# A mixture-of-experts and attention layer on one core: the setup of the weights laid out in another order

## The chip, the cores and the metric

One core of one Trainium2 chip. The metric is the device time of one execution in microseconds (us); smaller is better.

## The reference, cut to what matters

The input is 4 x 1024 tokens of 256 numbers in float32. Three residual steps follow each other: a mixture-of-experts layer of 32 experts (8 chosen for each token, further cut by a threshold), attention (16 heads of 16, 4 key/value heads, rotary tables), and the same mixture-of-experts layer again.

```
x = L0_attn_x
x = x + 0.5 * ffn(layernorm(x), gate_weight, gate_up_proj, down_proj)
x = x + attn(layernorm(x), Wq, Wk, Wv, Wo)
x = x + 0.5 * ffn(layernorm(x), gate_weight, gate_up_proj, down_proj)

logits = x @ gate_weight.T; probs = softmax(logits); top 8; keep until cumulated share 0.8; renormalise
for each expert: gu = x @ w_gu.T; g, u = split(gu); h = silu(g) * u; acc += h @ w_d.T * ce[:, None]
```

## The kernel before, in words

The 4096 tokens are 32 tiles of 128, held in `X` in SBUF (SBUF is the on-chip memory of 128 partitions) for the whole run. Four tiles make a group of 512 tokens, so there are 8 groups, and each is taken twice (two mixture layers), with attention between and beside them. A group is worked in two halves of 256 tokens, and a half in 12 slots. A slot `d` computes gate and up of two chunks of 128 hidden units (`gate_or_up`, 24 matmuls, L1015), then `down` of slot `d - 2` (12 matmuls, L1031). Between them ACT takes the tanh of the gate (`gate`, L578), DVE makes `gated` (L831) and `product` (L839), POOL multiplies by the tokens' combine weights (`weigh`, L508), ACT rounds to a high half (`high`, L585) and POOL subtracts for a low half (`low`, L513). Every product of matrices is made of float16 halves: high times high, high times low and low times high (`PASSES`). There are 384 slots. In the loop `for d in range(-1, SLOTS + 2)` each engine has its own list, written out by hand: slots, attention visits (from slot 64 on) and events. Semaphores alone tie the engines together.

Ahead of the loop stands the setup. The weights come as float32 and have to be scaled by a power of two and split into a float16 high half and a low half. In the order of the code:

- SP loads `st_gu` (gate and up weights, 12288 numbers on each partition) in two transfers, then all of `X` (L343, L344). ACT's queue loads the five small weights `st_g`, `st_q`, `st_k`, `st_v`, `st_o` and then the identity matrix (L553, L554). The down weights `st_d` (6144 numbers) have their place in the arena, a stretch of SBUF shared by staging and by the work buffers of the loop, and SP loads them (L348) only when gate/up and the small weights are split.
- DVE waits for the identity, takes the largest absolute value of each small weight (L679) and of the gate/up weights (L681). POOL reduces these over the partitions (L478, `partition_all_reduce`). DVE makes powers of two from them (`power_of_two`, L686 to L690) and factors for later (L700 to L704).
- `split_weights` (L693, L694) makes both halves on DVE: a `tensor_scalar` for the high one, a `scalar_tensor_tensor` for the low one. It runs for the small weights and then for all gate/up weights in one piece.
- The down weights follow: load, maximum (L714), reduction (L480), scale, both halves.
- Then come the memsets of `vb`, the norm of group 0 in four pieces (L738 to L750 and L734), with a power by POOL between them (`inverse_roots`, L485), the rounding of its rows (ACT L561, POOL L490), their transposition on PE (L966) and its copies on ACT (L566), the router's logits (L975), and routing in seven pieces on DVE (`route`, L763 to L799). SP writes the combine weights out and spreads them over the partitions (`write_combine`, L357, and `spread`, L368).
- PE waits for all splits before its first instruction (L1158 to L1161).

## Time and profile before

| | |
|---|---|
| median of 3 runs | 2420.05 us (2419.04 to 2420.05) |
| the profiled execution's own time | 2418.05 us |
| its span in the profile | 2416.3 us |
| PE busy (matmuls) | 2280.5 us, 94% |
| DVE busy | 1577.1 us, 65% |
| ACT busy | 1215.7 us, 50% |
| POOL busy | 1044.5 us, 43% |
| HBM traffic | 64.25 MB read, 12.85 MB written |

PE is TensorE, DVE is VectorE, ACT is ScalarE, POOL is GpSimd; SP only issues transfers. PEld is the loading of weights into PE, beside its matmuls. A line such as L1015 is the line of the kernel that issued the instruction. The span is the profiler's time from the first instruction to the last, and the execution's own time includes a little around it. Busy shares are averages over the whole span. Times in the timeline and in the chain count from the span's start.

### The profile page before, as it was taken

How to read it: one execution, taken by the hardware profiler on the slowest of the kernel's cores; microseconds unless marked ns; L12 is line 12 of the kernel's file. 1: busy time of each engine (PE TensorE's matmuls, PEld its weight loads, DVE VectorE, ACT ScalarE, POOL GpSimd, SP SyncE). 2: the span in 40 equal slices, each digit the busy share in tenths (PEclk: the TensorE clock that was granted, in tenths of full speed). 3: DMA queues.
4: the chain of work that ended last, by engine and by line, in shares of the span. 5: the costliest groups of instructions: out<-in, count | busy, mean ns of one | idle time of the engine just before them, and what ended most of it. 6: DMA issues, size and time to landing. Idle time of an engine off the chain costs nothing.

```text
span 2416.3 us, 48432 instructions
## 1 busy us (share of the span) xinstructions
PE 2280.5 (94%) x19616; PEld 1517.7 (63%) x19616; DVE 1577.1 (65%) x3099; ACT 1215.7 (50%) x1953; POOL 1044.5 (43%) x863
## 2 busy tenths in 40 slices
PE   0199999999999999999999999999999999999999
PEld 0188886555556556655555655555555655588887
DVE  6545556977777777777777777676776773345443
ACT  0123332156655656656666656666666665633332
POOL 0066664344343444344343433433433433366665
PEclk9999999999999999999999999999999999999999
DMA  5111112101110101111011011101101010011010
GB/s 191 54 36 29 34 37 58 29 14 31 31 30 19 48 21 37 31 25 41 11 37 37 18 33 28 32 3 39 31 21 30 13 29 19 11 37 28 19 37 19
DMA packets 96327, 80.24 MB, mean 33 GB/s; under 512 B 40292, under 2 KB 88676, under 8 KB 95720
## 3 DMA queue, kind: packets, MB, share of 16 engines
q1 hardware_dynamic: 95240, 76.09, 11.2%
q8 instruction: 155, 2.54, 0.4%
q10 hardware_dynamic: 864, 1.05, 0.1%
q14 instruction: 68, 0.56, 0.1%
HBM read 64.25 MB, written 12.85 MB: 32 GB/s over the span
## 4 chain that ended last, share of the span: by engine, by line
PE 90%; DVE 6%; DMA 2%; issue 1%; SPq 0%; POOL 0%; ACT 0%; ACTq 0%; POOLq 0%; DVEq 0%
PE PS L1015 41%; PE PS L1031 21%; PE PS L1043 11%; PE PS L1074 11%; PE PS L989 2%; DVE arena L854 1%; PE PS L1055 1%; PE PS L966 1%; PE PS L992 1%; PE PS L1113 1%; DMA ident<-ident_c 1%; PE PS L1099 1%; DVE WGU L694 1%; DVE amax L681 1%; PE PS L975 0%
## 5 line engine op out<-in xcount | busy, mean ns | idle before, releaser
L1015 PE MATMUL PS<-XT,WGU 128*128 128x256 f16 x9216 | 1117.6, 274 | 11.3 <-DVE arena L831 3.7
L1015 PEld LDWEIGHTS PS<-XT,WGU 128*128 128x128 f16 x9216 | 875.0, 98 | 242.7 <-issue 132.2
L513 POOL TENSOR_TENSOR arena<-arena 128x512 f16<-128x512 f32 x384 | 444.6, 1158 | 1199.8 <-ACT arena L585 1199.8
L854 DVE TENSOR_REDUCE arena<-PS 128x1 f32<-128x512 f32 x1024 | 658.2, 685 | 370.0 <-PE PS L1043 368.0
L608 ACT ACTIVATE arena<-PS,fac 128x512 f32<-128x512 f32 x1024 | 646.3, 684 | 235.8 <-PE PS L1055 234.5
L578 ACT ACTIVATE arena<-PS,fac 128x512 f32<-128x512 f32 x384 | 263.9, 687 | 763.0 <-PE PS L1015 763.0
L1031 PE MATMUL PS<-WD,arena 128*128 128x256 f16 x4608 | 569.4, 274 | 6.5 <-POOL arena L513 6.3
L1031 PEld LDWEIGHTS PS<-WD,arena 128*128 128x128 f16 x4608 | 432.4, 98 | 146.8 <-issue 89.5
L508 POOL TENSOR_TENSOR arena<-arena 128x512 f32<-128x512 f32 x384 | 487.3, 1269 | 49.3 <-DVE arena L839 27.7
L831 DVE SCALAR_TENSOR_TENSOR arena<-arena,PS 128x512 f32<-128x512 f32 x384 | 261.4, 681 | 295.9 <-ACT arena L578 295.4
L1043 PE MATMUL PS<-arena 48*128 48x512 f16 x1024 | 312.2, 382 | 7.2 <-DMA arena<-k_scratch 4.5
L1055 PE MATMUL PS<-arena 50*128 50x512 f16 x1024 | 308.9, 382 | 0.0
L839 DVE SCALAR_TENSOR_TENSOR arena<-arena,PS 128x512 f32<-128x512 f32 x384 | 263.8, 687 | 34.7 <-PE PS L1015 19.1
L1074 PE MATMUL PS<-arena 128*32 128x512 f32 x2048 | 272.9, 605 | 0.0
L585 ACT ACTIVATE arena<-arena 128x512 f16<-128x512 f32 x384 | 241.3, 628 | 12.2 <-POOL arena L508 12.2
L1043 PEld LDWEIGHTS PS<-arena 48*128 48x128 f16 x1024 | 58.3, 94 | 268.8 <-issue 205.6
L966 PE MATMUL PS<-ident,XS 128*128 128x128 f16 x384 | 30.2, 223 | 104.5 <-ACT XS L561 103.2
L966 PEld LDWEIGHTS PS<-ident,XS 128*128 128x128 f16 x384 | 25.1, 99 | 109.3 <-issue 106.4
L566 ACT ACTIVATE XT<-PS 128x1024 f16<-128x1024 f16 x48 | 49.1, 1023 | 54.1 <-PE PS L966 54.1
L1074 PEld LDWEIGHTS PS<-arena 128*32 128x32 f32 x2048 | 40.3, 108 | 54.0 <-issue 28.9
L1055 PEld LDWEIGHTS PS<-arena 50*128 50x128 f16 x1024 | 57.0, 94 | 21.0 <-issue 18.7
L490 POOL TENSOR_TENSOR XS<-XN,XS 128x1024 f16<-128x1024 f32 x24 | 51.1, 2129 | 4.7 <-ACT XS L561 4.7
(111 smaller groups left out, 842.6 us busy)
## 6 DMA issues: line engine op xcount, KB each, us to landing
arena<-ce_scratch SPq DMA_DIRECT2D x256, 128.0 KB, 3.2
arena<-wgu SPq DMA_DIRECT2D x2, 3072.0 KB, 14.9
arena<-q_scratch SPq DMA_DIRECT2D x96, 64.0 KB, 2.2
X<-x SPq DMA_DIRECT2D x1, 4096.0 KB, 31.2
arena<-ktab_c SPq DMA_DIRECT2D x16, 256.0 KB, 4.2
q_scratch<-arena SPq DMA_DIRECT2D x32, 128.0 KB, 1.7
out<-X SPq DMA_DIRECT2D x8, 512.0 KB, 3.0
arena<-wd SPq DMA_DIRECT2D x1, 3072.0 KB, 10.0
```

Of the source, the lines that this page charges most:

```text
L508: pool.tensor_tensor(t, t, c, ALU.mult).then_inc(w_done, 1)
L513: pool.tensor_tensor(hs[1][:, d % HS, :], tw[d % 2], hs[0][:, d % HS, :], ALU.subtract).then_inc(lo_done, 1)
L578: act.activation(z_f, PS[:, B_G, :], ACT.Tanh, scale=F_TANH).then_inc(z_done, 1)
L608: act.activation(pex[:, v % RING * 2 + half, :], PS[:, B_EXP + half, :], ACT.Exp, scale=F_EXP).then_inc(exp_done, 1)
L831: dve.scalar_tensor_tensor(z_f, z_f, 1.0, PS[:, B_G, :], ALU.add, ALU.mult).then_inc(v_done, 1)
L839: dve.scalar_tensor_tensor(tw[d % 2], z_f, G_U_UP, PS[:, B_U, :], ALU.mult, ALU.mult).then_inc(t_done, 1)
L854: dve.tensor_reduce(mx[:, half * REP * QT + c:half * REP * QT + c + 1], PS[:, B_MAX + half, :], AX_X, ALU.max).then_inc(max_taken, 1)
L1015: ins = pe.matmul(PS[:, b, j * HALF_G:(j + 1) * HALF_G], WGU[w][:, kt, part * CHUNKS + c + j, :], XT[r][:, k % 2, kt, half * HALF_G:(half ...
L1031: ins = pe.matmul(PS[:, B_Y, i * HID:(i + 1) * HID], hs[r][:, d % HS, at:at + P], WD[w][:, d % PER_HALF * 2 + j, :], start=(first and j == ...
L1043: pe.matmul(PS[:, B_MAX + half, :], qst[64 * par:64 * par + 48, slot, i, t * P:(t + 1) * P], kst[64 * par:64 * par + 48, slot, half * 512: ...
L1055: pe.matmul(PS[:, B_EXP + n % 2, :], kst[64 * par:64 * par + 50, slot, k * P:(k + 1) * P], qst[64 * par:64 * par + 50, slot, head // 2, ha ...
L1074: ins = pe.matmul(PS[32 * head:32 * head + 32, B_O, :], vst[:, u % 2, k, :], pex[:, (2 * q + r // 2) % RING * 2 + r % 2, :], start=(k == 0 ...
```

## The change

The setup and its waits are written anew; the loop over the slots keeps its instructions.

- SP loads the rows of groups 0 and 1 first (1 MB), then gate/up in two transfers with a semaphore each, then the down weights at once, into the part of `X` whose rows come last. The remaining rows (3 MB) are loaded when the down weights are split. The identity is now first on ACT's queue.
- The arena is carved in another order: the work buffers of the slots (`CB`, `z_f`, `tw`, `hs`) stand at its end, behind the staging of the gate/up weights.
- Maxima, reductions and scales are made in three rounds: small weights, gate/up, down.
- The norm of group 0 and the first piece of its routing stand ahead of the gate/up maximum; the other pieces are between the maxima.
- High halves, but for the router's, are made on ACT (`activation` with Identity and a scale); low halves stay on DVE.
- The gate/up weights are split in four pieces of three slots each, an instruction for each of the two row blocks. ACT makes piece 0, the down weights, and pieces 1 to 3. DVE makes piece 0 and the down weights ahead of the loop, and pieces 1 to 3 behind the products of slots 0 to 2.
- PE waits for each piece where it needs it. The `vb` memsets and the transfers of `kneg` move into the loop, to slot 4.

```diff
-        (cb_f, z_f, t_all, hi_f, lo_f, kcos, ksin, rb, qo_hi, qo_lo, vb_f,
-         qst_f, kst_f, vst_f, pe_f, oT, otok_f, osp_hi, osp_lo, mx, rd_f, ml, mlT) = carve(
-            [(2 * 4 * HALF_G, F32), (GROUP, F32), (2 * GROUP, F32), (HS * GROUP, F16), (HS * GROUP, F16)]
-            + [(GROUP, F32)] * 3 + [(2 * GROUP, F16)] * 2 + [(GT * KV * 32, F32)]
+        assert n_d == (TILES - 2 * GT) * HID
+        st_d = X[:, 2 * GT:, :].rearrange("p t h -> p (t h)")
+        in_pieces = st_gu.rearrange("p (k t q n) -> p q k t n", k=KT, t=2, q=PIECES)
+        hi_pieces, lo_pieces = (w.rearrange("p k (t q c) m -> p q k t (c m)", t=2, q=PIECES) for w in WGU)
+
+        (kcos, ksin, rb, qo_hi, qo_lo, vb_f, qst_f, kst_f, vst_f, pe_f, oT, otok_f, osp_hi, osp_lo, mx, rd_f, ml, mlT,
+         cb_f, z_f, t_all, hi_f, lo_f) = carve(
+            [(GROUP, F32)] * 3 + [(2 * GROUP, F16)] * 2 + [(GT * KV * 32, F32)]
             + [(QKV * 2 * SEQ, F16), (QKV * SEQ, F16), (2 * QT * 32, F32), (RING * 2 * 512, F32), (512, F32),
                (QT * P, F32), (QT * P, F16), (QT * P, F16), (2 * REP * QT, F32), (QT * REP, F32),
...
@@ -338,17 +345,12 @@
         @block.sync
         def _(sp):
+            x_rows = x.rearrange("(i p) h -> p i h", p=P)
+            sp.dma_start(X[:, 0:2 * GT, :], x_rows[:, 0:2 * GT, :]).then_inc(x_in, 16)
             for k in range(KT):
                 n = n_gu // KT
-                sp.dma_start(st_gu[:, k * n:(k + 1) * n], wgu[:, k * n:(k + 1) * n]).then_inc(gu_in, 16)
-            sp.dma_start(X[:, :, :], x.rearrange("(i p) h -> p i h", p=P)).then_inc(x_in, 16)
-
-            sp.wait_ge(gu_split, 1)
-            sp.wait_ge(small_split, 1)
+                sp.dma_start(st_gu[:, k * n:(k + 1) * n], wgu[:, k * n:(k + 1) * n]).then_inc(gu_in[k], 16)
             sp.dma_start(st_d, wd).then_inc(d_in, 16)
-            sp.wait_ge(d_split, 1)
-            for par in range(2):
-                sp.dma_start(kst[64 * par + 48:64 * par + 50, :, :], kneg_c).then_inc(const_rows, 16)
             def write_combine(k):
...
+                if d == PIECES:
+                    sp.wait_ge(gu_split, PIECES)
+                    for par in range(2):
+                        sp.dma_start(kst[64 * par + 48:64 * par + 50, :, :], kneg_c).then_inc(const_rows, 16)
                 if d % 6 == 2 and (d + 4) % PER_GROUP and d + 4 < SLOTS:
                     spread((d + 4) // 6)
...
             pool.wait_ge(consts_set, 1)
-            pool.wait_ge(amax_all, 1)
-            pool.partition_all_reduce(wmax[:, :], amax[:, :], P, ABSMAX).then_inc(wmax_all, 1)
-            pool.wait_ge(amax_d, 1)
-            pool.partition_all_reduce(wmax[:, S_D:S_D + 1], amax[:, S_D:S_D + 1], P, ABSMAX).then_inc(wmax_d, 1)
+            pool.wait_ge(amax_small, 1)
+            pool.partition_all_reduce(wmax[:, S_G:N_SCALES], amax[:, S_G:N_SCALES], P, ABSMAX).then_inc(wmax_small, 1)
...
+            pool.wait_ge(amax_gu, 1)
+            pool.partition_all_reduce(wmax[:, S_GU:S_GU + 1], amax[:, S_GU:S_GU + 1], P, ABSMAX).then_inc(wmax_gu, 1)
+            pool.wait_ge(amax_d, 1)
+            pool.partition_all_reduce(wmax[:, S_D:S_D + 1], amax[:, S_D:S_D + 1], P, ABSMAX).then_inc(wmax_d, 1)
             for d in range(-1, SLOTS + 2):
...
         def _(act):
+            act.dma_start(ident[:, :], ident_c).then_inc(const_in, 16)
             for v, src in ((st_g, wg), (st_q, wq), (st_k, wk), (st_v, wv), (st_o, wo)):
                 act.dma_start(v, src).then_inc(small_in, 16)
-            act.dma_start(ident[:, :], ident_c).then_inc(const_in, 16)
             def rows_high(i):
...
                     take_tokens(n, j, bank)
-            act.wait_ge(scales_set, 1)
             rows_high(0)
+            act.wait_ge(scales_small, 1)
+            for i, v, w in ((S_Q, st_q, WQ), (S_K, st_k, WK), (S_V, st_v, WV)):
+                act.activation(flat(w[0]), v, ACT.Identity, scale=up[:, i:i + 1])
+            act.activation(flat(WO[0]), st_o, ACT.Identity, scale=up[:, S_O:S_O + 1]).then_inc(small_hi, 1)
             take_rows(0, 0, 0, B_O)
             take_rows(0, 0, 1, B_O)
             exponentials(0)
+            act.wait_ge(scales_gu, 1)
+            for q in range(PIECES):
+                for k in range(KT):
+                    ins = act.activation(hi_pieces[:, q, k], in_pieces[:, q, k], ACT.Identity, scale=up[:, S_GU:S_GU + 1])
+                ins.then_inc(gu_hi, 1)
+                if q == 0:
+                    act.wait_ge(scales_d, 1)
+                    act.activation(flat(WD[0]), st_d, ACT.Identity, scale=up[:, S_D:S_D + 1]).then_inc(d_hi, 1)
             for d in range(-1, SLOTS + 2):
                 k, s = divmod(d, PER_GROUP)
                 if d + 1 < SLOTS:
...
-            dve.wait_ge(small_in, 16 * len(small))
-            for s, v in small:
-                link(dve.tensor_reduce(amax[:, s:s + 1], v, AX_X, ALU.max, apply_absolute_value=True))
-            dve.wait_ge(gu_in, 32)
-            dve.tensor_reduce(amax[:, S_GU:S_GU + 1], st_gu, AX_X, ALU.max, apply_absolute_value=True)\
-               .then_inc(amax_all, 1)
+            def amax_of(i, v):
...
+
             mul = ALU.mult
-            link(dve.tensor_scalar(F_TANH, wmax[:, S_GU:S_GU + 1], 0.5 / XW, None, mul))
-            link(dve.tensor_scalar(F_LOGIT, wmax[:, S_G:S_G + 1], 1 / XW, None, mul))
-            link(dve.scalar_tensor_tensor(F_EXP, wmax[:, S_Q:S_Q + 1], HD ** -0.5 / 64, wmax[:, S_K:S_K + 1],
-                                          mul, mul))
-            link(dve.scalar_tensor_tensor(F_O, wmax[:, S_V:S_V + 1], 2.0 ** -18, wmax[:, S_O:S_O + 1], mul, mul))
-            link(split_weights(S_G, st_g, flat(WG[0]), flat(WG[1])))
...
-
-            link(dve.scalar_tensor_tensor(F_T, wmax[:, S_GU:S_GU + 1], 2.0 ** -10, wmax[:, S_GU:S_GU + 1], mul, mul))
-            dve.tensor_scalar(F_Y, F_T, wmax[:, S_D:S_D + 1], None, mul).then_inc(scales_set, 1)
-            split_weights(S_D, st_d, flat(WD[0]), flat(WD[1])).then_inc(d_split, 1)
-            dve.wait_ge(scales_set, 1)
-            dve.wait_ge(d_split, 1)
+            def split_small():
+
+                dve.wait_ge(small_hi, 1)
+                link(low_weights(S_Q, st_q, flat(WQ[0]), flat(WQ[1])))
+                link(low_weights(S_K, st_k, flat(WK[0]), flat(WK[1])))
+                link(low_weights(S_V, st_v, flat(WV[0]), flat(WV[1])))
+                low_weights(S_O, st_o, flat(WO[0]), flat(WO[1])).then_inc(small_split, 1)
+
+            def split_piece(q):
+
+                dve.wait_ge(gu_hi, q + 1)
+                for k in range(KT):
+                    ins = low_weights(S_GU, in_pieces[:, q, k], hi_pieces[:, q, k], lo_pieces[:, q, k])
+                ins.then_inc(gu_split, 1)
...
-            dve.memset(vb[:, :, :, HD:HD + 1], 1.0).then_inc(vb_set, 1)
-            dve.wait_ge(vb_set, 2)
+            dve.wait_ge(small_in, 16 * len(small))
+            for i, v in small[:-1]:
+                link(amax_of(i, v))
+            amax_of(*small[-1]).then_inc(amax_small, 1)
             dve.wait_ge(x_in, 16)
-            for piece in range(4):
-                norm(0, 0, piece)
-            for piece in range(7):
-                route(0, piece, B_O)
+            norm(0, 0, 0)
+            norm(0, 0, 1)
+            dve.wait_ge(wmax_small, 1)
+            link(power_of_two(S_G, N_SCALES))
+            dve.tensor_scalar(flat(WG[0]), st_g, up[:, S_G:S_G + 1], None, mul).then_inc(scales_small, 1)
+            dve.wait_ge(scales_small, 1)
+            low_weights(S_G, st_g, flat(WG[0]), flat(WG[1])).then_inc(g_split, 1)
+            link(dve.tensor_scalar(F_LOGIT, wmax[:, S_G:S_G + 1], 1 / XW, None, mul))
+            norm(0, 0, 2)
+            norm(0, 0, 3)
+            link(dve.scalar_tensor_tensor(F_EXP, wmax[:, S_Q:S_Q + 1], HD ** -0.5 / 64, wmax[:, S_K:S_K + 1],
+                                          mul, mul))
+            link(dve.scalar_tensor_tensor(F_O, wmax[:, S_V:S_V + 1], 2.0 ** -18, wmax[:, S_O:S_O + 1], mul, mul))
+            split_small()
+            route(0, 0, B_O)
+            dve.wait_ge(gu_in[0], 16)
+            link(dve.tensor_reduce(amax[:, S_GU:S_GU + 1], st_gu[:, 0:n_gu // KT], AX_X, ALU.max,
+                                   apply_absolute_value=True))
+            dve.wait_ge(gu_in[1], 16)
+            link(dve.tensor_reduce(pad[:, :], st_gu[:, n_gu // KT:], AX_X, ALU.max, apply_absolute_value=True))
+            dve.tensor_tensor(amax[:, S_GU:S_GU + 1], amax[:, S_GU:S_GU + 1], pad[:, :], ALU.max).then_inc(amax_gu, 1)
+            for piece in range(1, 4):
+                route(0, piece)
+            dve.wait_ge(wmax_gu, 1)
+            link(power_of_two(S_GU, S_GU + 1))
+            link(dve.tensor_scalar(F_TANH, wmax[:, S_GU:S_GU + 1], 0.5 / XW, None, mul))
+            dve.scalar_tensor_tensor(F_T, wmax[:, S_GU:S_GU + 1], 2.0 ** -10, wmax[:, S_GU:S_GU + 1], mul, mul)\
+               .then_inc(scales_gu, 1)
+            dve.wait_ge(d_in, 16)
+            amax_of(S_D, st_d).then_inc(amax_d, 1)
+            for piece in range(4, 7):
+                route(0, piece)
+            dve.wait_ge(wmax_d, 1)
+            link(power_of_two(S_D, S_D + 1))
+            dve.wait_ge(scales_gu, 1)
+            dve.tensor_scalar(F_Y, F_T, wmax[:, S_D:S_D + 1], None, mul).then_inc(scales_d, 1)
+            split_piece(0)
+            dve.wait_ge(scales_d, 1)
+            dve.wait_ge(d_hi, 1)
+            low_weights(S_D, st_d, flat(WD[0]), flat(WD[1])).then_inc(d_split, 1)
             for d in range(-1, SLOTS + 2):
                 k, s = divmod(d, PER_GROUP)
                 if d % PER_HALF == 1 and d > 1:
@@ -930,6 +973,13 @@
                 if d + 1 < SLOTS:
                     gated(d + 1)
                     product(d + 1)
+                if d + 2 < PIECES:
+                    split_piece(d + 2)
+                if d == PIECES:
+                    dve.memset(vb_f, 0.0).then_inc(vb_set, 1)
+                    dve.wait_ge(vb_set, 1)
+                    dve.memset(vb[:, :, :, HD:HD + 1], 1.0).then_inc(vb_set, 1)
+                    dve.wait_ge(vb_set, 2)
                 if (d, 1) in VISIT:
                     visit(VISIT[d, 1])
                 if len(EVENTS[d]) > 1:
...
                 b, done = ((B_G, g_done), (B_U, u_done))[part]
                 if d:
                     pe.wait_ge((v_done, t_done)[part], d)
...
                 first, last = d % PER_HALF == 0, d % PER_HALF == PER_HALF - 1
...
-            pe.wait_ge(const_rows, 32)
             transpose_rows(0, 0, B_O)
             pe.wait_ge(xt_hi, 1)
             transpose_rows(0, 1, B_O)
             pe.wait_ge(xt_lo, 1)
+            pe.wait_ge(g_split, 1)
             logits(0, B_O)
```

**ACT, from its first arithmetic to slot 1.** A row is the line, the operation, the tiles written and read, and their size. Before (L561 is the rounding of group 0's rows, L566 the transposed copies, L571 the router's exponential, L578 tanh, L585 a slot's high half):

```order
L561 ACT_TABLE_LOAD
L561 ACTIVATE XS<-XN 128x1024
L566 ACTIVATE XT<-PS 128x1024 x2
L571 ACTIVATE pr<-ld,fac 128x4x32
L578 ACTIVATE arena<-PS,fac 128x512 x2
L585 ACTIVATE arena<-arena 128x512
```

Now (L572, L577, L582, L589 and L596 are those five):

```order
L572 ACT_TABLE_LOAD
L572 ACTIVATE XS<-XN 128x1024
L641 ACTIVATE WQ<-arena,up 128x1024
L641 ACTIVATE WK<-arena,up 128x256
L641 ACTIVATE WV<-arena,up 128x128
L642 ACTIVATE WO<-arena,up 128x512
L577 ACTIVATE XT<-PS 128x1024 x2
L582 ACTIVATE pr<-ld,fac 128x4x32
L649 ACTIVATE WGU<-arena,up 128x2x768 x2
L653 ACTIVATE WD<-X,up 128x6144
L649 ACTIVATE WGU<-arena,up 128x2x768 x6
L589 ACTIVATE arena<-PS,fac 128x512 x2
```

Four small high halves now stand between the rows' rounding and their transposed copies, and nine large ones between the router's exponential and the first tanh.

**DVE, from the last factor to slot 3** (L836 is `gated`, L844 `product`). Now:

```order
L962 TENSOR_SCALAR fac<-fac,wmax 128x1
L711 SCALAR_TENSOR_TENSOR WGU<-arena,up,WGU 128x2x768 x2
L711 SCALAR_TENSOR_TENSOR WD<-X,up,WD 128x6144
L836 SCALAR_TENSOR_TENSOR arena<-arena,PS 128x512
L844 SCALAR_TENSOR_TENSOR arena<-arena,PS 128x512
L711 SCALAR_TENSOR_TENSOR WGU<-arena,up,WGU 128x2x768 x2
L836 SCALAR_TENSOR_TENSOR arena<-arena,PS 128x512
L844 SCALAR_TENSOR_TENSOR arena<-arena,PS 128x512
```

Two more pieces follow in the same way, behind slots 1 and 2. Before, all splitting (L693, L694) stood ahead of the norm and routing, and slots followed each other with nothing between.

**POOL, from its start to slot 0.** An `ISA` row without tiles is an instruction that changes the loaded library; one with tiles is the reduction over the partitions. In brackets is what an instruction waits for. Before (L508 is `weigh`):

```order
L478 ISA
L478 ISA wmax<-amax 128x8 [waits amax_all,consts_set]
L480 ISA wmax<-amax 128x1 [waits amax_d]
L485 ISA
L485 TENSOR_TENSOR rs<-var,mhalf 128x4 [waits var_ready]
L490 TENSOR_TENSOR XS<-XN,XS 128x1024 [waits xs_hi]
L508 TENSOR_TENSOR arena<-arena 128x512 [waits cb_in0,t_done]
```

Now (L515 is `weigh`):

```order
L487 ISA
L487 ISA wmax<-amax 128x6 [waits amax_small,consts_set]
L492 ISA
L492 TENSOR_TENSOR rs<-var,mhalf 128x4 [waits var_ready]
L497 TENSOR_TENSOR XS<-XN,XS 128x1024 [waits xs_hi]
L534 ISA
L534 ISA wmax<-amax 128x1 [waits amax_gu]
L536 ISA wmax<-amax 128x1 [waits amax_d]
L515 ISA
L515 TENSOR_TENSOR arena<-arena 128x512 [waits cb_in0,t_done]
```

The power (L485, now L492) stood behind both reductions and now stands between the first and the second, and the changes of library are four where they were two.

## Rows read from the trace of the kernel before

**Rows 1.** The page: shares of the engines, and the chain by engine.

```profile
PE 2280.5 (94%) x19616; PEld 1517.7 (63%) x19616; DVE 1577.1 (65%) x3099; ACT 1215.7 (50%) x1953; POOL 1044.5 (43%) x863
...
PE 90%; DVE 6%; DMA 2%; issue 1%; SPq 0%; POOL 0%; ACT 0%; ACTq 0%; POOLq 0%; DVEq 0%
```

**Rows 2.** Two stretches: us, busy us (instructions) by engine, clock, DMA share, GB/s.

```profile
0.00:131.59 131.59, 17.67 (x125) 13.11 (x126) 74.32 (x102) 8.00 (x10) 8.73 (x13) 0.96 0.34 120
131.59:2416.30 2284.71, 2262.79 (x19492) 1504.64 (x19490) 1502.80 (x2997) 1207.68 (x1943) 1035.80 (x851) 1.00 0.11 28
```

**Rows 3.** The chain in order of time (start us, us, what).

```profile
3.65 18.63 DMA ident<-ident_c
...
25.57 12.96 DVE amax L681
...
52.97 13.03 DVE WGU L694
...
76.10 6.56 DVE amax L714
...
135.67 2.62 PE PS L1015 x24
```

**Rows 4.** DMA queues (q1 SP, q10 ACT), 6 to 14 us: packets, MB, share.

```profile
q1 hardware_dynamic: 130, 2.80, 81.5%
q10 hardware_dynamic: 130, 0.47, 14.3%
```

**Rows 5.** Stretches as in rows 2; the last two figures: DMA share, GB/s.

```profile
1.00:2.00 1.00, 0.00 (x0) 0.00 (x0) 0.07 (x2) 0.00 (x0) 0.00 (x0) 1.00 0.85 197
...
14.00:16.00 2.00, 0.00 (x0) 0.00 (x0) 0.00 (x0) 0.00 (x0) 0.00 (x0) 1.00 1.02 436
...
28.00:30.00 2.00, 0.00 (x0) 0.00 (x0) 2.00 (x1) 0.00 (x0) 0.00 (x0) 1.00 1.10 348
```

**Rows 6.** Timeline, DVE's setup: start us, us, engine line op out<-in [idle <-releaser].

```profile
22.57 2.97 DVE L679 TENSOR_REDUCE amax<-arena 128x1 f32<-128x64 f32 x5
...
39.18 0.17 DVE L686 TENSOR_SCALAR wmax<-wmax 128x8 f32<-128x8 f32 x1 [0.66 <-POOL wmax L478]
```

**Rows 7.** Timeline, norm of group 0 and its high rows.

```profile
95.23 1.41 DVE L738 BATCH_NORM_STATS2 stats<-X 128x6 f32<-128x256 f32 x4
...
98.45 0.16 DVE L747 TENSOR_TENSOR nw<-rs 128x4 f32<-128x4 f32 x1 [1.19 <-POOL rs L485]
...
99.25 1.38 DVE L734 TENSOR_SCALAR XN<-X,mv,rstd 128x256 f32<-128x256 f32 x4
100.71 1.28 ACT L561 ACT_TABLE_LOAD   x1 [100.71 <-DVE XN L734]
102.00 1.06 ACT L561 ACTIVATE XS<-XN 128x1024 f16<-128x1024 f32 x1
```

**Rows 8.** Timeline, ACT's high half of slot 0.

```profile
126.93 0.63 ACT L585 ACTIVATE arena<-arena 128x512 f16<-128x512 f32 x1 [7.30 <-POOL arena L508]
```

**Rows 9.** Timeline, transposed copy and routing of group 0.

```profile
104.25 1.02 ACT L566 ACTIVATE XT<-PS 128x1024 f16<-128x1024 f16 x1 [1.19 <-PE PS L966]
...
110.08 0.29 DVE L770 TENSOR_TENSOR pr<-pr,r 128x128 f32<-128x128 f32 x1
...
115.22 0.31 DVE L799 STREAM_TRANSPOSE combT<-comb 128x128 f32<-128x128 f32 x1
```

**Rows 10.** Timeline, the same multiplication in the loop.

```profile
2297.49 1.24 DVE L770 TENSOR_TENSOR pr<-pr,r 128x128 f32<-128x128 f32 x1
```

**Rows 11.** Timeline of POOL, second reduction and power.

```profile
82.75 0.38 POOL L480 PARTITION_ALL_REDUCE wmax<-amax  x1 [43.60 <-DVE amax L714]
97.35 1.06 POOL L485 TENSOR_TENSOR rs<-var,mhalf 128x4 f32<-128x4 f32 x1 [14.22 <-DVE var L744]
```

**Rows 12.** Stretches as in rows 2 (third figure from the end: clock).

```profile
118.00:120.00 2.00, 2.00 (x12) 1.39 (x10) 0.34 (x1) 0.69 (x1) 0.00 (x0) 0.50 0.15 25
```

**Rows 13.** Timeline, PE's first `down`.

```profile
128.84 2.74 PE L1031 MATMUL PS<-WD,arena 128*128 128x256 f16 x12 [4.66 <-POOL arena L513]
```

56 lines of the change are left out of this document (27 added, 29 removed).

## The prediction

> **What bounds the kernel now.** First read the engines' shares and the chain that ended last. TensorE (PE) is busy 94% of the span and carries 90% of the chain [rows 1]. The two stretches then say where the other tenth lies: up to 131.59 us PE has worked 17.67 us of 131.59, behind it 2262.79 of 2284.71 [rows 2]. So the time is a setup of some 131 us, in which PE waits, and a stream of matmuls that is full. The change touches only the setup, and the stream issues the same matmuls after it, so I ask one thing: how much earlier does the stream begin? The chain in order of time shows the setup as one file of steps: the constant's landing at 22.28, the maximum of the gate/up weights, their two halves, the wait for the down weights, their maximum, their halves, and only then the first group's rows [rows 3]. Its last row is my mark: gate and up of slot 4 start at 135.67. They sit on a chain of matmuls from the first `down` on; in the changed kernel I look for the same slot.
>
> **When the small weights are in (call it S).** Before, `ident` is issued at 3.65 and lands 18.63 us later [rows 3]. The two queues share engines: from 6 to 14 us each served 130 packets, but 2.80 MB went to SP's queue and 0.47 to ACT's [rows 4]. One small packet goes per large one of the 3 MB loads. Now SP's first load is 1 MB of rows, in packets of 1 KB like the later part of the 4 MB load, which runs at 348 GB/s [rows 5]. ACT's five weights and `ident` are another 1.05 MB. Together 2.1 MB at 348 GB/s are 6.0 us; data flow from within the second us on [rows 5], say 1.6, so the lower end is S = 7.6. ACT's last issue comes at about 3.7 and some of its packets may still meet the large ones. A packet of those is a 24 KB row of one partition, 0.9 us at a sixteenth of 436 GB/s [rows 5]. If all of `wo`'s share (128 rows, 8 for each of 16 engines) waits for one each, that is 7.2 us more, an upper end of about 15; the old 22.5 is the rival's. I take S = 9, near the lower end, since the byte count of the rows is nearly that of the small weights and they end together.
> The skill's rule speaks against this. The Trainium skill (DMA: Bandwidth & Descriptors, Queues, rings and completion order) says an engine changes between queues only after a packet of some 9 to 17 descriptors. By that the large loads could hold the small queue for a whole turn, and S would stay near the old one. The trace counts one for one [rows 4] and decides for me; the rule is rival A.
>
> **The chain from S on, step by step** (where I can, durations are distances between rows, so that gaps are in them).
> DVE: five small maxima, 22.57 to 25.57, 3.0 [rows 3, 6]; norm pieces 0 and 1, from 95.23 to 97.26 (98.45 less the idle 1.19), 2.0 [rows 7]; four scale steps of 0.17 and some 0.04 between them, 0.85 [rows 6], and three more small ones for `WG` and a factor, about 0.25 each: S+6.7. Norm pieces 2 and 3, 98.45 to 100.63, 2.2 [rows 7]: S+8.9. ACT: table load and high rows, 2.35 and a start of 0.1 [rows 7]: S+11.3. Then the four small high halves. ACT's price per column comes from two rows, 1024 columns in 1.06 and 512 in 0.63 [rows 7, 8]: 0.84 ns per column on 0.2 us. So 1024, 256, 128 and 512 columns cost about 2.6: S+13.9. From the first transposed copy, 104.25, to the multiplication of routing piece 1, 110.08, are 5.8 [rows 9]; the exponential and two small steps, 1.0, belong behind piece 0, so its end is 4.8 after the copy's start: S+18.7. DVE's four low halves (1920 columns at 13.03/12288, 1.06 ns [rows 3], and four starts, 3.0) lie beside it, and so are free.
> The gate/up maximum is 12.95 in one piece [rows 3]; in two, with one more joining step, 13.3: S+32.0. Its bytes are in by 7.6 plus 6.3 MB at the 409 GB/s of [rows 4], 23 us, and it starts its second half at S+25, so the load is hidden; the down weights follow by 31 and are wanted at S+36. Routing pieces 1 to 6 took from 109.5 to 115.53, 6.0 [rows 9], about half of it ahead of the gate/up scales and half behind the down maximum; scales and two factors 1.3; down maximum 6.6 [rows 3]; scales and `F_Y` 1.0: S+46.9.
> Now ACT is what is late. It holds, in its order, `WD` high (6144 columns, 5.4) and six half pieces of `WGU` (1536 columns, 1.5 each, 9.0) ahead of the first tanh: S+61.4. DVE's first piece (a quarter of 13.03, 3.3) and `WD` low (6.6) end at S+59 and are hidden by it. The combine weights' way out and back ends by S+56: before, from 115.53 to slot 0's high half at 126.93 are 11.4, with 1.27 of `weigh` among them [rows 8, 9]. Tanh, gated and product are 0.69 each, like all of their kind: S+63.6.
> Then DVE alternates: piece 1, slot 1, piece 2, slot 2, piece 3, slot 3. A piece is 3.3 and a slot's two products 1.45. And here is a cost that the setup's rows don't show, since POOL stood idle then. The same multiplication takes 0.29 alone and 1.24 beside POOL's work [rows 9, 10]: two SBUF inputs on DVE wait while POOL has the port. Each piece is two such instructions and meets POOL's `weigh` and `low`. Ends: none, or two holds of 1.25 for each piece; I take one, since `weigh` is asked for as a piece's first half starts and so comes between the halves. 3 x (3.3+1.25) + 2 x 1.45 = 16.6: S+80.2, and slot 3's gated product ends at S+80.9. Slot 4 starts at S+81.0, against 135.67. Without anything more that is 54.7 - S, 45.7 us earlier.
>
> **POOL's reload** is what the change adds. Its order now goes reduction, power, subtraction, reduction, reduction, weighing, with a library instruction at each change: three behind the first, where there was one. Only the first of them is exposed: the first reduction ends at S+3.7 (0.66 passes for DVE between a maximum and the scale step [rows 6]), the power is wanted by S+5.1 and its result by DVE at S+6.7. The trace of before has this change of code inside a gap: from 83.13 to 97.35 POOL shows nothing, and then the power waits only for DVE's `var` [rows 11]. So its length is between nothing and 14.2. In between I have no nearer row and take the middle, 7: power ready at S+3.7+7+1.1, 5.1 us later than DVE wants it. Ends: 0 and 12.3. The other two lie in DVE's 13 us maximum and in ACT's 14 us of high halves; if they took over 14 us they would show too.
> The Trainium skill (GPSIMD Engine Reference, Instruction dispatch) gives about 6 us for the first call of freshly loaded code; an estimate from that page is 4.1 us lost instead of 5.1, and the forecast would be 1 us lower.
>
> **Clock.** Before, at 116 to 120 us PE's granted clock was 0.50 (1.2 GHz) and the first `down`, 12 matmuls, took 2.74 behind an idle time of 4.66, where 24 matmuls take 2.62 at 135.67 [rows 3, 12, 13]. In the changed kernel PE works in pieces between DVE's long instructions up to slot 4, so it may begin at 1.2 GHz: 0 to 2.8 lost, I take 1.5.
> **Costless.** The 3 MB of remaining rows are issued at S+59, about 9 us, while group 2's norm comes at slot 33, over 100 us later. SP's next transfer, the second spread, queues behind them but is wanted only by slot 6, some 20 us on. The two memsets move to slot 4 (0.6 us of DVE, which is idle 2.5 us a slot). `kneg` is wanted at slot 64.
>
> **Sum.** 45.7 - 5.1 - 1.5 = 39.1 us off the profiled execution's own 2418.05, which is 2379. The median of the runs is 2 us above that execution, so the forecast is 2381. By best ends (S 7.6, no reload, no holds, no clock loss) it is 2420 - 50.8 = 2369; by worst (15, 12.3, two holds, 2.8) 2420 - 20.9 = 2399.
>
> **Rivals.**
> A. The small weights stay late (S 22.5), as the cited rule has it: 13.5 us of the gain go, 2394.5. For it stand 18.63 us for 32 KB; against it the packet counts. Chance 0.08.
> B. Reload and holds cost nothing: 5.1 and 3.8 more, 2372. For it: nothing of either is seen in the setup before. Against: the row of 1.24. Chance 0.24.
> C. Not what it says: the overlap is undone because all high halves stand on ACT ahead of the first tanh, and ACT needs 0.84 ns per column in copies without a scale from memory. If pointer scales or the split access made ACT's column cost 1.25 ns, the 15360 columns of this stretch cost 6.3 us more: 2387. Chance 0.10.
> D. Slower than before. The buffers of every slot (`CB`, `z_f`, `tw`, `hs`) move to the arena's end. If ACT, DVE or POOL met there so that each of the 384 slots grew by 0.15 us, 57.6 us would be added: 2381 + 57.6 = 2439. It decides from 0.10 us per slot on. Against it: a slot in the stream is 3.93 us of pure PE and the other engines idle over 1 us in each. Chance 0.02.
> E. My forecast, with the sizes about as taken: 0.55, and 0.01 for no change to be seen.
>
> **Numbers.** Predicted 2381, the likeliest case. The range 2369 to 2395 takes in B, C and A and leaves out the far end of reload and D. A measurement here tells 0.2%, 4.8 us, from no change. A, B, C and E all are faster by 25 us or more; slower is D. Faster 0.97, same 0.01, slower 0.02.
>
> **What would show it.** Right: first small maximum at 8 to 11 us; a POOL gap between reduction and power with DVE waiting for it 4 to 6 us; WGU maximum ending near 46; ACT solid with high halves up to about 75, tanh right behind; DVE's half pieces 1 to 3 at 2.2 us in the mean against 1.65 for piece 0; slot 4 near 95 to 97 and the stretch behind it as long as now. Wrong: a small maximum at 22, a stream longer than 2281 from slot 4 on, a wait of PE for `gu_split` or of POOL for the combine weights after slot 0.

## The result, and the profile after

| | before | changed kernel |
|---|---|---|
| median of the runs, us | 2420.0 (2419.04 to 2420.05) | 2397.55 (2396.93 to 2397.75) |
| ratio, 95% interval | | 0.9908 [0.9891, 0.9925] |
| profiled execution, us (span) | 2418.05 (2416.3) | 2396.93 (2395.1) |
| small weights in (S), us | 22.57 | 31.12 |
| gate and up of slot 4 start at, us | 135.67 | 113.56 |

The changed kernel is 22.4 us faster. The prediction was a gain of 39, and its range ended at 2395: it missed by 16.6 us, on the side of too much.

First the shares and the chain by engine, from the page of the changed kernel; [rows 1] are those of before. TensorE has a point more of the span and of the chain, and ACT, at 0% of the chain before, is now in it with 1%: the high halves that it took over.

```profile
PE 2280.0 (95%) x19616; PEld 1517.8 (63%) x19616; DVE 1568.7 (65%) x3106; ACT 1235.5 (52%) x1966; POOL 1052.1 (44%) x864
...
PE 91%; DVE 5%; DMA 1%; ACT 1%; issue 1%; SPq 0%; POOL 0%; ACTq 0%; POOLq 0%; DVEq 0%
```

Then the same cut as in the prediction, setup and stream, with slot 4's start as the border. The first two lines are the changed kernel, in the columns of [rows 2]:

```profile
0.00:113.56 113.56, 20.43 (x161) 15.62 (x161) 66.52 (x109) 28.78 (x25) 18.21 (x16) 0.95 0.38 139
113.56:2395.10 2281.54, 2259.55 (x19456) 1502.20 (x19456) 1502.17 (x2998) 1206.74 (x1941) 1033.93 (x849) 1.00 0.11 28
```

and this is the kernel before, behind its own slot 4:

```profile
135.67:2416.30 2280.63, 2258.71 (x19457) 1501.02 (x19454) 1501.43 (x2995) 1206.47 (x1941) 1032.97 (x848) 1.00 0.11 28
```

The stream took 2281.54 us against 2280.63: it is the same but for 0.9 us. Of the 21.2 us between the spans, 22.1 lie ahead of slot 4. (135.67 is the chain's row; by the timeline slot 4 of the kernel before began at 135.51, and the two figures would be 0.8 and 21.9.) So the question stays where the prediction put it, in the setup.

The chain in order of time (start, us, what) shows the new setup from end to end. It answers to [rows 3].

```profile
3.54 27.47 DMA arena<-wo
...
36.03 5.66 issue
...
86.06 8.79 ACT WGU L649 x6
...
113.56 2.79 PE PS L1069 x24
```

Its first step is the finding: a load of 256 KB, issued at 3.54, that lands at 31.0. Before, `ident`, the last of the small transfers to land, took 18.63. The timeline of VectorE (DVE) shows that nothing stood ahead of it; DVE waited 27.81 us for this one load. In the same rows stand the other steps that the prediction priced ([rows 6, 7, 11] are those of before).

```profile
4.10 1.28 ACT L572 ACT_TABLE_LOAD   x1 [4.10 <-issue]
31.12 2.97 DVE L700 TENSOR_REDUCE amax<-arena 128x1 f32<-128x64 f32 x5 [27.81 <-DMA arena<-wo]
34.31 0.40 POOL L487 PARTITION_ALL_REDUCE wmax<-amax  x1 [33.49 <-DVE amax L700]
41.69 1.05 POOL L492 TENSOR_TENSOR rs<-var,mhalf 128x4 f32<-128x4 f32 x1 [6.98 <-issue]
42.85 0.16 DVE L752 TENSOR_TENSOR nw<-rs 128x4 f32<-128x4 f32 x1 [5.44 <-POOL rs L492]
53.03 6.54 DVE L943 TENSOR_REDUCE amax<-arena 128x1 f32<-128x6144 f32 x1
80.52 3.54 DVE L711 SCALAR_TENSOR_TENSOR WGU<-arena,up,WGU 128x1536 f16<-128x1536 f32 x2
80.64 5.42 ACT L653 ACTIVATE WD<-X,up 128x6144 f16<-128x6144 f32 x1 [7.26 <-DVE fac L962]
85.96 8.89 ACT L649 ACTIVATE WGU<-arena,up 128x1536 f16<-128x1536 f32 x6
94.76 0.66 ACT L589 ACTIVATE arena<-PS,fac 128x512 f32<-128x512 f32 x1
96.20 5.08 PE L1069 MATMUL PS<-XT,WGU 128*128 128x256 f16 x24 [7.77 <-DVE arena L836]
96.78 4.55 DVE L711 SCALAR_TENSOR_TENSOR WGU<-arena,up,WGU 128x1536 f16<-128x1536 f32 x2
```

**Why the load is so late.** Two views of the transfer queues (q1 is SP's, q10 ACT's; packets, MB, share of the engines' time) tell it. While the rows come in, from 2.6 to 4.6 us, ACT's queue gets next to nothing:

```profile
q1 hardware_dynamic: 610, 0.62, 91.3%
q10 hardware_dynamic: 11, 0.00, 0.5%
```

And then, from 6 to 14 us, the two share packet by packet, whatever a packet's size (in the first single microseconds of it, 20 to 14 and 16 to 15):

```profile
q1 hardware_dynamic: 122, 2.83, 82.3%
q10 hardware_dynamic: 115, 0.47, 14.3%
```

So it goes on from 14 to 29 us:

```profile
q1 hardware_dynamic: 288, 6.29, 98.1%
q10 hardware_dynamic: 285, 0.24, 4.8%
```

From 29 to 30 only ACT's queue has packets left (125).

The transfers of the start, with their size and the time from issue to landing (from the same view), give the rest:

```profile
X<-x SPq DMA_DIRECT2D x1, 1024.0 KB, 5.9
...
arena<-wq ACTq DMA_DIRECT2D x1, 512.0 KB, 13.7
arena<-wo ACTq DMA_DIRECT2D x1, 256.0 KB, 27.5
arena<-wk ACTq DMA_DIRECT2D x1, 128.0 KB, 20.9
arena<-wv ACTq DMA_DIRECT2D x1, 64.0 KB, 27.5
```

The rows landed 5.9 us after their issue, and SP's short packets ended with them. Behind them on SP's queue stand 9 MB in rows of 24 KB. The two halves of the gate/up weights are 128 such rows each and the down weights 128 more, 24 turns for each of 16 engines. `wq`, `wk` and `wv` are 24 small turns for each engine too, and each small one waits for a large one. The turns begin as the last rows go over, at about 6 us. From 6 to 14 a turn takes 16 engines x 8 us / 122 packets, 1.05 us; later, beside rows of 1 and 0.5 KB, it is shorter, and all 24 are over at 29, 0.96 us each in the mean. Only then is `wo`, behind them, free of large neighbours, and it is in at 31. In the kernel before, only 16 large turns per engine stood at the head of SP's queue; then came rows in short packets, and the small queue got through at 22.5 us. Loading the rows first and the down weights straight behind gate/up is what made the small weights later than ever. Why ACT's queue got next to nothing beside the rows is a second question, and no run here answers it.

### The profile page after: what moved, and what is told of

Same layout as the page of the kernel before. It is cut to its first block, busy times and chain, and to the rows that moved or that the text cites. A ratio compares the mean times of both kernels' runs of the same rounds, so it can differ in the third digit from the quotient of the medians.

```text
span 2395.1 us, 48463 instructions
## 1 busy us (share of the span) xinstructions
PE 2280.0 (95%) x19616; PEld 1517.8 (63%) x19616; DVE 1568.7 (65%) x3106; ACT 1235.5 (52%) x1966; POOL 1052.1 (44%) x864
## 3 DMA queue, kind: packets, MB, share of 16 engines
q1 hardware_dynamic: 95256, 76.09, 11.3%
q10 hardware_dynamic: 864, 1.05, 0.1%
## 4 chain that ended last, share of the span: by engine, by line
PE 91%; DVE 5%; DMA 1%; ACT 1%; issue 1%; SPq 0%; POOL 0%; ACTq 0%; POOLq 0%; DVEq 0%
PE PS L1069 42%; PE PS L1087 21%; PE PS L1099 11%; PE PS L1130 11%; PE PS L1041 2%; DMA arena<-wo 1%; DVE arena L859 1%; PE PS L1111 1%; PE PS L1016 1%; PE PS L1044 1%; PE PS L1171 1%; PE PS L1157 1%; PE PS L1025 0%; DVE arena L836 0%; DVE amax L700 0%
## 5 line engine op out<-in xcount | busy, mean ns | idle before, releaser
L589 ACT ACTIVATE arena<-PS,fac 128x512 f32<-128x512 f32 x384 | 263.9, 687 | 762.1 <-PE PS L1069 762.1
L515 POOL TENSOR_TENSOR arena<-arena 128x512 f32<-128x512 f32 x384 | 492.0, 1281 | 50.2 <-DVE arena L844 49.0
L836 DVE SCALAR_TENSOR_TENSOR arena<-arena,PS 128x512 f32<-128x512 f32 x384 | 261.2, 680 | 284.1 <-ACT arena L589 283.7
L844 DVE SCALAR_TENSOR_TENSOR arena<-arena,PS 128x512 f32<-128x512 f32 x384 | 263.7, 687 | 33.8 <-PE PS L1069 17.9
L596 ACT ACTIVATE arena<-arena 128x512 f16<-128x512 f32 x384 | 241.4, 629 | 5.7 <-POOL arena L515 5.6
L577 ACT ACTIVATE XT<-PS 128x1024 f16<-128x1024 f16 x48 | 49.1, 1023 | 53.5 <-PE PS L1016 53.5
L1111 PEld LDWEIGHTS PS<-arena 50*128 50x128 f16 x1024 | 56.8, 94 | 21.0 <-issue 18.7
```

The source lines that it names most:

```text
L515: pool.tensor_tensor(t, t, c, ALU.mult).then_inc(w_done, 1)
L589: act.activation(z_f, PS[:, B_G, :], ACT.Tanh, scale=F_TANH).then_inc(z_done, 1)
L836: dve.scalar_tensor_tensor(z_f, z_f, 1.0, PS[:, B_G, :], ALU.add, ALU.mult).then_inc(v_done, 1)
L844: dve.scalar_tensor_tensor(tw[d % 2], z_f, G_U_UP, PS[:, B_U, :], ALU.mult, ALU.mult).then_inc(t_done, 1)
L1111: pe.matmul(PS[:, B_EXP + n % 2, :], kst[64 * par:64 * par + 50, slot, k * P:(k + 1) * P], qst[64 * par:64 * par + 50, slot, head // 2, ha ...
```

## The experiments

Each kernel is the changed kernel but for the edit shown. Times are medians, and each ratio is against the kernel before on the same chip (medians there: 2420.16, 2419.3 and 2419.91 in the three sets). "Library change" is the time from the end of POOL's reduction over the small weights to the start of its power, where nothing else holds the power back; beside it stands the share of time that the transfer engines were busy in that gap. In best_b and best_c it is the change the other way, from the end of POOL's subtraction to the start of that reduction.

| kernel | S | library change (engines busy) | slot 4 | median | ratio, 95% |
|---|---|---|---|---|---|
| changed kernel | 31.12 | 6.98 (0.00) | 113.56 | 2397.55 | 0.9908 [0.9891, 0.9925] |
| small_sp | 9.43 | 12.00 (0.99) | 96.89 | 2379.59 | 0.9836 [0.9821, 0.985] |
| hold_wd | 23.89 | 10.19 (0.50) | 109.54 | 2393.4 | 0.9892 [0.9875, 0.9908] |
| rows_after | 22.94 | 8.29 (0.44) | 106.68 | 2389.54 | 0.9877 [0.9863, 0.9892] |
| short_packets | 17.60 | 10.58 (0.94) | 103.65 | 2386.65 | 0.9864 [0.9849, 0.9878] |
| late_large | 9.12 | 7.57 (0.00) | 92.79 | 2376.61 | 0.9823 [0.9809, 0.9838] |
| high_on_dve | 31.18 | 7.67 (0.00) | 122.98 | 2408.59 | 0.9955 [0.9939, 0.9972] |
| pieces_ahead | 31.09 | 7.20 (0.00) | 116.11 | 2399.96 | 0.9921 [0.9907, 0.9936] |
| norm_first | 31.14 | hidden | 102.30 | 2386.24 | 0.9862 [0.9847, 0.9877] |
| act_order | 31.20 | 7.06 (0.00) | 110.93 | 2394.49 | 0.9897 [0.9882, 0.9912] |
| halves | 31.33 | 7.24 (0.00) | 109.41 | 2392.9 | 0.9891 [0.9876, 0.9905] |
| best_b | 12.06, behind the norm | 8.50 (1.02), hidden | 80.02 | 2363.69 | 0.9771 [0.9756, 0.9785] |
| best_c | 11.82, behind the norm | 8.64 (1.04), hidden | 74.89 | 2359.03 | 0.9751 [0.9735, 0.9768] |

The first four ask why the small weights are late.

**small_sp: the small weights on SP's queue, between the rows and gate/up.**

```diff
-            for v, src in ((st_g, wg), (st_q, wq), (st_k, wk), (st_v, wv), (st_o, wo)):
-                act.dma_start(v, src).then_inc(small_in, 16)
...
             sp.dma_start(X[:, 0:2 * GT, :], x_rows[:, 0:2 * GT, :]).then_inc(x_in, 16)
+            for v, src in ((st_g, wg), (st_q, wq), (st_k, wk), (st_v, wv), (st_o, wo)):
+                sp.dma_start(v, src).then_inc(small_in, 16)
```

> The five small weights are issued on SP's queue, between the first rows and the gate/up weights; nothing else differs from the changed kernel. Theory TURNS (each of the 16 engines serves ACT's queue one packet for each packet of SP's queue, so the small weights pay one 24 KB packet of 0.95 us for each of their own): the small weights now stand ahead of the large ones in one queue, the last of them is in at 8 to 10 us (31.1 in the changed kernel), everything behind shifts by 21 to 23 us and the time is 2374 to 2377. Rival BYTES (the small weights are late because the engines are full and all loads share their rate by bytes): they would still be in at 20 us or later, 2386 or more. Rival NEXT (another wait takes the place of this one, the gate/up load above all): in early, but DVE then waits for the gate/up weights and the time stays over 2380.

S fell from 31.12 to 9.43, near the prediction's 9, and the time by 18.0 us, to 2.6 us above the expected 2374 to 2377. That is less than S did, and the timeline says why: POOL's change of library grew from 6.98 to 12.00, and DVE's wait for the power from 5.44 to 10.46.

```profile
9.43 2.97 DVE L700 TENSOR_REDUCE amax<-arena 128x1 f32<-128x64 f32 x5 [6.01 <-DMA arena<-wo]
12.62 0.40 POOL L489 PARTITION_ALL_REDUCE wmax<-amax  x1 [11.81 <-DVE amax L700]
25.02 1.05 POOL L494 TENSOR_TENSOR rs<-var,mhalf 128x4 f32<-128x4 f32 x1 [12.00 <-issue]
26.18 0.16 DVE L752 TENSOR_TENSOR nw<-rs 128x4 f32<-128x4 f32 x1 [10.46 <-POOL rs L494]
```

**hold_wd: the down weights wait on SP until the small ones are in.**

```diff
+            sp.wait_ge(small_in, 80)
             sp.dma_start(st_d, wd).then_inc(d_in, 16)
```

> SP waits for the small weights before it issues the down weights. TURNS: 16 large packets for each engine are left instead of 24, wq and wk take their turns beside them, wv and wo go alone behind them: small weights in at 22.5 to 24.5 us, time 2389 to 2391. Rival ROWS (the first rows' 1024 short packets took the turns of the small queue and the rest follows from that): in at 31 as now, time 2397. DVE must not wait for the down weights, which land at about 33 and are wanted at 62.

S came to 23.89 as worked out from packets: with 16 large turns per engine in place of 24, `wo` gets through when they are over. The time missed its expectation by 2.4 us, for the library change took 10.19: now the down weights came in beside it.

**rows_after: the part "rows first" undone.**

```diff
-            sp.dma_start(X[:, 0:2 * GT, :], x_rows[:, 0:2 * GT, :]).then_inc(x_in, 16)
             for k in range(KT):
...
+            sp.dma_start(X[:, 0:2 * GT, :], x_rows[:, 0:2 * GT, :]).then_inc(x_in, 16)
             sp.dma_start(st_d, wd).then_inc(d_in, 16)
```

> The first rows are loaded behind the gate/up weights and ahead of the down weights: the part 'first rows loaded first' is undone. TURNS: wgu's 16 large packets pass beside wq and wk, and wv and wo take their turns beside the rows' short packets of 0.05 us, as in the kernel before: small weights in at 22 to 24, time 2388 to 2391, so that the part undone costs 7 to 9 us. Rival BYTES: in at 31 or at least 28, time 2395 or more.

S is 22.94, near that of the kernel before, and the time 8.0 us lower than the changed kernel's, both as expected. Put first, the rows cost 8 us, since nothing used them early: in this kernel too DVE takes the small maxima before the norm.

**short_packets: gate/up in 8 transfers and the down weights in 4, rows of 6 KB in place of 24.**

```diff
-                n = n_gu // KT
-                sp.dma_start(st_gu[:, k * n:(k + 1) * n], wgu[:, k * n:(k + 1) * n]).then_inc(gu_in[k], 16)
-            sp.dma_start(st_d, wd).then_inc(d_in, 16)
+                for j in range(4):
+                    at, n = k * (n_gu // KT) + j * (n_gu // 8), n_gu // 8
+                    sp.dma_start(st_gu[:, at:at + n], wgu[:, at:at + n]).then_inc(gu_in[k], 16)
+            for j in range(4):
+                at, n = j * (n_d // 4), n_d // 4
+                sp.dma_start(st_d[:, at:at + n], wd[:, at:at + n]).then_inc(d_in, 16)
```

DVE's waits for these loads count to 64 in place of 16.

> The gate/up weights go in eight transfers of 1536 columns and the down weights in four, so that a packet is 6 KB instead of 24 KB; order and bytes are the same. TURNS: a turn costs 0.24 us, the 32 packets for each engine of wq, wk, wv and wo are through after 8 to 10 us: small weights in at 14.5 to 17.5 us, time 2381 to 2385. BYTES: bytes and rates are the same, in at 29 to 31, time 2395 to 2398.

The queues from 6 to 14 us: still near one for one, at four times the packets.

```profile
q1 hardware_dynamic: 483, 2.58, 78.6%
q10 hardware_dynamic: 442, 0.74, 24.4%
```

No order was changed here, only the length of a row, and S fell by 13.5 us, to 17.60, at the upper edge of what was expected. So a small queue pays for each of its packets with one packet of the neighbour, and the price is that packet's length. Together the four settle what the 24 turns cost. None of them tells why ACT's queue got next to nothing beside the first rows, which hold_wd and this kernel show again (605 to 18 and 607 to 24 packets from 2.6 to 4.6 us). The time again came 3 us above what S alone gives, and above the expected 2381 to 2385, and again the library change was long (10.58).

The next asks what makes it long.

**late_large: small_sp, and SP waits for the power's result ahead of gate/up.**

```diff
+            sp.wait_ge(rs_ready, 1)
             for k in range(KT):
```

> As small_sp, but SP also waits for POOL's power of group 0 (rs_ready) before it issues the gate/up and down weights. Theory RELOAD (POOL's change of library between the first reduction and the power is itself a load, and it is slower the fuller the transfer engines are: 6.98 us from the reduction's end to the power in the changed kernel, 12.00 in small_sp): with the engines empty it takes 7 us or less, the power starts at 20 us instead of 25.0, and although the large weights start 18 us later they are still in before DVE wants them, so the time falls by 5 us to 2374 to 2376. Rival FIXED (the gap has another cause, POOL's own work, and does not depend on transfers): gap 12, power at 25, time 2379 to 2380 or more. Rival LATE: the gate/up weights become the bound, DVE waits for them, time over 2380.

With no transfer on the engines during the change it takes 7.57, in place of 12.00 (7 or less was expected):

```profile
20.28 1.05 POOL L495 TENSOR_TENSOR rs<-var,mhalf 128x4 f32<-128x4 f32 x1 [7.57 <-issue]
...
38.83 6.55 DVE L947 TENSOR_REDUCE pad<-arena 128x1 f32<-128x6144 f32 x1 [0.67 <-DMA arena<-wgu]
```

The second line is the cover: gate/up, issued only at 21.4, is late by 0.67 us. Against small_sp the change is 4.4 us shorter and S 0.3 earlier; less the 0.67 that is 4.1, and slot 4 starts 4.1 earlier. The medians differ by 3.0, to 0.6 above the expected 2374 to 2376. The table's middle column goes with it: 6.98 to 7.67 beside idle engines in six kernels, 8.29 and 10.19 beside half-busy ones, 10.58 and 12.00 beside full ones. What the engines carry for POOL in that time isn't in the trace; that their load lengthens the change is shown by this run against small_sp. It doesn't follow for every change of library: the one the other way took only 8.50 and 8.64 beside full engines (best_b, best_c), and no run has it exposed beside idle ones.

Three look at the back of the setup.

**high_on_dve: the high halves back on DVE.** The four of the small weights, the eight half pieces of gate/up and that of the down weights leave ACT; in each piece it reads

```diff
-                dve.wait_ge(gu_hi, q + 1)
+                for k in range(KT):
+                    link(dve.tensor_scalar(hi_pieces[:, q, k], in_pieces[:, q, k], up[:, S_GU:S_GU + 1], None, ALU.mult))
                 for k in range(KT):
```

> The part 'high halves on ACT' is undone in the changed kernel: small, down and gate/up high halves are made by DVE ahead of their low halves, in the same four pieces. The gate/up and down part of DVE grows by 6.6 and 3.4 us, ACT's 14.3 us ahead of the first tanh go. Theory: up to slot 0 both cost the same (DVE then has 15 us of splitting where ACT had 14.3), and only pieces 1 to 3, now longer by 1.65 us each and by a hold of up to 1.2, show: slot 4 at 119 to 121 instead of 113.6, time 2402 to 2405. Rival (ACT's high halves are hidden anyway, or DVE was not the bound): within 1.5 us of 2397.5.

```profile
97.62 2.95 DVE L717 TENSOR_SCALAR WGU<-arena,up 128x1536 f16<-128x1536 f32 x2
...
100.60 4.44 DVE L700 SCALAR_TENSOR_TENSOR WGU<-arena,up,WGU 128x1536 f16<-128x1536 f32 x2
```

It costs 11.0 us, more than the 4.5 to 7.5 expected. From slot 1 to slot 4 are 25.95 us in place of 17.36, 8.6 more; another 0.8 was lost before slot 1 (97.03 against 96.20), and 1.7 behind slot 4, whose 24 matmuls took 4.46 instead of 2.79 (the granted clock is 0.50 from 124 to 126 us, behind an idle time of 4.43) and put slot 5 5.6 us behind it, not 3.93. A piece's high half also takes 2.95 beside POOL against 2.07 alone, which the expectation had not counted. So of the three parts that were undone alone this one is worth most.

**pieces_ahead: all four pieces split before the first slot's work.**

```diff
+            for q in range(1, PIECES):
+                split_piece(q)
             for d in range(-1, SLOTS + 2):
...
-                if d + 2 < PIECES:
-                    split_piece(d + 2)
```

> DVE makes the low halves of pieces 1 to 3 ahead of the loop instead of behind the products of slots 0 to 2; nothing else differs from the changed kernel. The holds by POOL go (3.3 us a piece instead of 4.55), but slot 0 starts 10 us later and the slots then need their own latency. Theory: gated product of slot 0 at 102.7 instead of 95.4, slot 4 at 115 to 117 instead of 113.6, time 2398.5 to 2401, so that the interleaving is worth 1 to 3 us only. Rival (the interleaving is worth what it seems, the 10 us of splitting that it takes out of the way): 2404 or more.

```profile
92.89 10.46 DVE L711 SCALAR_TENSOR_TENSOR WGU<-arena,up,WGU 128x1536 f16<-128x1536 f32 x6
```

Three pieces together take 10.46, 3.5 each, against 4.55 beside POOL. Splitting in pieces between the slots is worth only 2.4 us: what it lets PE do early it gives back in the holds and in slots that still come at DVE's pace.

**act_order: the down weights' high half behind the third piece of gate/up, not behind the first.**

```diff
-                if q == 0:
+                if q == 2:
                     act.wait_ge(scales_d, 1)
```

> Only ACT's order: pieces 0 to 2 of the gate/up weights ahead of the down weights, piece 3 behind. In the changed kernel ACT waits 7.3 us for the down scales with three pieces still to make. Theory: ACT is done at 89 instead of 94.8, the down weights' high half a little later, and DVE's low half of the down weights becomes the last: slot 0's gated product at 92.5 to 94.5 instead of 95.4, time 2394.5 to 2396.5. Rival (ACT's order is hidden): within 0.7 us of 2397.5.

```profile
86.30 6.62 DVE L711 SCALAR_TENSOR_TENSOR WD<-X,up,WD 128x6144 f16<-128x6144 f32 x1 [2.10 <-ACT WD L653]
92.83 0.68 DVE L836 SCALAR_TENSOR_TENSOR arena<-arena,PS 128x512 f32<-128x512 f32 x1
```

3.1 us less than the changed kernel, at the lower edge of what was expected: ACT makes three pieces (70.49 to 79.39) without waiting for the down maximum. Now DVE's low half of the down weights ends last, and the first product comes 2.6 us earlier (92.83 against 95.45), as does slot 4.

The last four ask how much of the late S, the library change and the holds can be hidden.

**norm_first: the norm of group 0 and its power ahead of the small maxima.**

```diff
-            dve.wait_ge(small_in, 16 * len(small))
...
             dve.wait_ge(x_in, 16)
-            norm(0, 0, 0)
-            norm(0, 0, 1)
+            for piece in range(4):
+                norm(0, 0, piece)
+            dve.wait_ge(small_in, 16 * len(small))
...
             inverse_roots(0)
             rows_low(0)
+            pool.wait_ge(amax_small, 1)
+            pool.partition_all_reduce(wmax[:, S_G:N_SCALES], amax[:, S_G:N_SCALES], P, ABSMAX).then_inc(wmax_small, 1)
```

On ACT the transposed copies move ahead of the small high halves.

> Only the norm of group 0 (with POOL's power and subtraction, ACT's rounding and the two transposed copies) is put ahead of the small weights' maxima; the small weights stay on ACT's queue and come at 31 us as in the changed kernel. Theory: the 5.4 us in which DVE waits for the power behind the change of library, the norm's 3.7 us and the 2 us in which the copies wait on ACT leave the chain, since all of it fits between the rows (7 us) and the small weights (31): routing piece 0 at 41.5 to 43 instead of 52.5, time 2386 to 2388. Rival: POOL's change of library back to the reduction is not done when the small maxima are (34 us), and DVE waits there instead: time 2390 or more.

```profile
8.94 1.01 POOL L490 TENSOR_TENSOR rs<-var,mhalf 128x4 f32<-128x4 f32 x1 [8.12 <-DVE var L749]
...
41.79 6.54 DVE L941 TENSOR_REDUCE amax<-arena 128x1 f32<-128x6144 f32 x1
```

S is still 31.14, yet the gate/up maximum starts at 41.79 instead of 53.03, and the time falls by 11.3 us. Here the early rows are used at last: norm, power and rows are made while the small weights crawl in, and the library change falls into DVE's wait for them. No run puts the norm first with the rows behind gate/up. In rows_after they land at 24.4 us; an estimate from these rows (norm to the end of POOL's subtraction 8.7, change of library 8.5) puts the reduction at some 41.6 there, against 34.24 here.

**halves: pieces 1 to 3 in six halves, one behind each of slots 0 to 5, in place of three wholes behind slots 0 to 2.**

```diff
-                if d + 2 < PIECES:
-                    split_piece(d + 2)
+                if d + 1 < (PIECES - 1) * KT:
+                    split_half(d + 1 + KT)
```

> Pieces 1 to 3 of DVE's low halves are dealt out as six half pieces behind the products of slots 0 to 5 instead of three pieces behind slots 0 to 2 (each piece is still ready before its slot; the vb memsets and kneg two slots later). In the changed kernel slots 1 to 4 start 5.8 us apart, bound by DVE (1.45 + 4.3), where the stream has 3.93. Theory HOLD (a DVE instruction with two SBUF inputs and POOL's work wait for each other, 1 to 1.25 us for a half piece): slots 4.0 to 4.4 us apart, 3 to 5 us won, time 2392.5 to 2394.5. Rival: the latency from tanh to the next gate sets 5.8 whatever DVE does: 2397 or more.

```profile
97.23 1.81 DVE L711 SCALAR_TENSOR_TENSOR WGU<-arena,up,WGU 128x1536 f16<-128x1536 f32 x1
...
105.22 2.78 PE L1077 MATMUL PS<-XT,WGU 128*128 128x256 f16 x24
...
109.41 2.78 PE L1077 MATMUL PS<-XT,WGU 128*128 128x256 f16 x24
```

A half piece and a slot's two products fit into 4.2 us, near the 3.93 of a slot in the stream, so slots run almost at PE's pace from slot 3 on. 4.7 us less than the changed kernel. Of the six half pieces five took 1.81 and one 2.10, against 2.27, the mean half of a whole one. The two halves of the changed kernel's piece at 96.78 tell why (nanoseconds, shortest/median/longest, then the first and the last start):

```profile
L711 DVE SCALAR_TENSOR_TENSOR WGU<-arena,up,WGU x2: 1810/2316/2821, 96.8 to 98.5; 128x1536 f16<-128x1536 f32 x2
```

POOL's `weigh` runs from 96.95 to 99.71. The first half starts ahead of it and takes 1.81, as each half does where POOL has no work (piece 0, at 80.52); the second starts while `weigh` is at work and takes 2.82. So a piece has one hold of 1.0, on its second half. In halves the five that took 1.81 start ahead of an instruction of POOL or in the last 0.2 us of one, and the one of 2.10, at 108.77, starts 0.5 us before a `weigh` ends (107.99 to 109.26). POOL waits too: `weigh` takes 2.76 beside the changed kernel's pieces and 1.27 without them.

**best_b and best_c: the parts together.** best_b has small_sp, norm_first and act_order, and takes both gate/up maxima ahead of the small scales and the down maximum right behind the gate/up scales, so that DVE follows the loads. best_c adds halves.

> A version built on these readings: small weights on SP's queue behind the first rows; norm of group 0 complete, with POOL's power and subtraction, ahead of the first reduction; both gate/up maxima ahead of the small weights' scales; down maximum right behind; ACT makes pieces 0 to 2 of the gate/up weights before the down weights. POOL's change of library now lies beside the gate/up maxima. Expected: gate/up maximum done at 31 to 32 us (it is bound by the weights' landing at 24), scales at 34, slot 0's gated product at 60 to 63 instead of 95.4, time 2362 to 2366. If the change of library takes 12 us from the subtraction's end at 16 to 19, it just fits; if it takes more, DVE waits for the first reduction and 2 to 5 us are lost.

> best_b with the half pieces of the run halves. Both together: 2358.5 to 2361, if what the half pieces win in the changed kernel is won here too.

```profile
16.66 6.55 DVE L930 TENSOR_REDUCE amax<-arena 128x1 f32<-128x6144 f32 x1 [1.64 <-DMA arena<-wgu]
...
23.94 0.40 POOL L534 PARTITION_ALL_REDUCE wmax<-amax  x1 [8.50 <-issue]
```

These rows are best_b's. The library change of 8.50 lies inside a maximum that DVE takes anyway, and nobody waits for it. How much that is worth shows in the first 31 us, in which both kernels load the same bytes at the same mean rate (372 GB/s; the columns are those of [rows 2]). The changed kernel:

```profile
0.00:31.00 31.00, 0.00 (x0) 0.00 (x0) 0.44 (x6) 1.28 (x1) 0.29 (x5) 1.00 0.91 372
```

and best_c:

```profile
0.00:31.00 31.00, 2.02 (x16) 1.55 (x16) 20.81 (x35) 4.39 (x4) 4.17 (x9) 1.00 0.92 372
```

DVE did 0.44 us of work there in the one and 20.81 in the other. best_c, at 2359.03, is 38.5 us under the changed kernel and 60.9, 2.5%, under the one before.

## Why the prediction was wrong

**The step that failed: "I take S = 9, near the lower end, since the byte count of the rows is nearly that of the small weights and they end together."** They did not end together. While the rows came, 610 of their packets stood against 11 small ones, so that at 6 us, when the rows were over, only `ident` and `wg` had gone over. Sharing by bytes is not what happened, but one packet for one isn't either in this stretch: the small weights are 48 packets for each engine and the rows 64, so by that rule too, an estimate from these counts, they would have gone over beside the rows. The cause of the 610 to 11 stays open. What it led to is clear: the rest met the large rows, 24 turns of 0.96 us. S was 31.12, 22.1 us later. The upper end of 15 let only `wo` meet the large packets, and the rival A went no further than the old 22.5; neither counted `wq`, `wk` and `wv`, whose 24 turns stand ahead of `wo`. The price of the turns was in [rows 4]: 130 packets in 8 us on 16 engines are 0.98 us for a turn, 24 turns 23.6 us, and with the rows' 6 us ahead of them 29.6. That the small queue would stand still beside the rows was in no row. The time fell between rival A and the kernel before. Rival A is nearest in kind, small weights held up by large loads, but by turns of one for one and not by the rule that it cited.

Of the rest, each step measured from S, what the prediction had and what came:

- **First routing piece.** S+23.8 with the reload (18.7 and 5.1); measured S+21.9. ACT's table load, 1.3 of it, had left the chain: it stands at 4.10 now, before there was work, where it stood behind the wait for the norm in [rows 7]. The four small high halves took 2.3 (46.02 to 48.36); the prediction's own price makes 2.4 of them, not the 2.6 that it added.
- **POOL's reload**, 7 for the change and 5.1 for DVE: 6.98 and 5.44. That is luck: 7 was the middle of a range from nothing to 14.2, and it fits idle transfer engines, which the late S brought about. With S early it is 12.00 and 10.46. The Trainium skill (GPSIMD Engine Reference, Instruction dispatch) gives some 6 us; beside these runs it is a floor, not a price.
- **Gate/up maximum** 13.3: 13.2. The load was hidden as said.
- **`F_Y`, the last of the scales,** S+52.0 with the reload: S+49.4, the same 1.9 and 0.7 more.
- **ACT's high halves**, 14.4 for `WD` and `WGU`: 14.1 (80.64 to 94.76). Rival C, a higher price per column with a scale from memory, has fallen: 6144 columns took 5.42.
- **The rounds.** From slot 0's product to slot 4's start 17.4; measured 16.8 (from DVE's piece at 96.78 to 113.56). A piece took 4.55 beside POOL, as taken, but as 3.54 alone and a hold of 1.0, where 3.3 and 1.25 stood. The hold sits on the second half, between the halves as the prediction had it. Both parts of rival B, no reload and no holds, have fallen.
- **Clock**, 1.5 lost: nothing at slot 4. The stretches tell it (third figure from the end is the granted clock):

```profile
98.00:100.00 2.00, 2.00 (x11) 1.39 (x10) 2.00 (x2) 0.94 (x2) 1.72 (x1) 0.50 1.10 381
...
102.00:104.00 2.00, 2.00 (x19) 1.80 (x20) 2.00 (x2) 0.49 (x1) 1.62 (x2) 1.00 1.13 272
```

  PE began slot 1 at 1.2 GHz, its 24 matmuls in 5.08 instead of 2.79, after an idle time of 7.77. But DVE's piece behind it is 4.55 long and slot 2 comes 5.79 later, so the slow matmuls lie beside it. At slot 2 the clock is 2.4 GHz again.
- **The stream**, 0.9 us longer, not 57.6: rival D has fallen. The buffers at the arena's end cost at most that.

Summed up: slot 4 was to come at S + 81.0 + 5.1 + 1.5 = S+87.6 and came at S+82.4. The steps behind S were 5.2 us too dear; S was 22.1 too early; with 0.9 in the stream that is 17.8 of the 17.9 by which the profiled execution's 2396.93 lies over 2379. small_sp, with S at 9.43, landed at 2379.59 where 2381 was forecast for S = 9. That isn't the prediction come true in all its terms, since the reload took 5 us more there and the steps behind 5 us less.

Taking the changed kernel's parts one at a time: high halves on ACT are worth 11.0 us, pieces between the slots 2.4, the rows first cost 8.0. If the parts add up, the rest of the 22.4, some 17, belongs to all that was not undone alone, above all what stands ahead of and beside the maxima now (norm, routing and small splits). That last figure is a difference, not a run.

## What to carry to other kernels

- Where both queues were at work in these traces they took turns by packets, one for one (122 to 115, 483 to 442), but not beside the first rows (610 to 11). Put small loads that are wanted first ahead of large ones in the same queue, or keep the neighbour's rows short; count the turns ahead of the last small packet, not bytes.
- Loading something early pays only if it is used early: rows first cost 8 us against rows behind gate/up, and with the norm put ahead of the small maxima, so that the early rows were used, the kernel gained 11.3.
- Look for the order in which an engine's waits fall: a library change of 7 to 12 us costs nothing where the other engines have work of their own in front of them.

## What the runs showed of the hardware that was not expected

- In the first microseconds a transfer of 1 KB rows got 610 packets while the second queue got 11, though from 6 to 14 us the two took turns at 122 to 115. `wg`, issued at 1.18, was among those that waited. Whether that queue was held back or its rows weren't yet on their way isn't told apart here. The Trainium skill (DMA: Bandwidth & Descriptors, Queues, rings and completion order) lets an engine stay with a queue for a packet of some 9 to 17 descriptors. The trace doesn't agree where it can be counted: beside 24 KB rows it shows one row per turn, down to single microseconds (16 to 15 from 7 to 8 us), and in short_packets 483 to 442 over 8 us.
- POOL's change of library from the reduction to the power took 6.98 to 7.67 us beside idle transfer engines and up to 12.00 beside full ones; the change back took 8.50 and 8.64 beside full ones.
- ACT's table load moved 97 us forward, from behind the wait at 100.71 to 4.10, though the diff has no line that moves it. It does take out the wait for `scales_set` ahead of ACT's first instruction; whether that is the reason no run tells.
- A DVE instruction with one SBUF tensor input is held beside POOL too: two of 1536 columns took 2.95 against 2.07 alone.
- A DVE instruction that starts ahead of POOL's isn't held, and the one that starts beside it is: 1.81 and 2.82 for the two halves of one piece, 1.81 each alone.
